# Attention: scores for the maxima six steps ahead in place of eight, and a batch's first keys rotated and split ahead of other work

## The chip, the core and the metric

The kernel runs on one core of a Trainium2 chip. Its engines each run their own instructions in order: TensorE (PE; PEld is its weight load), VectorE (DVE), ScalarE (ACT), GpSimd (POOL) and SyncE (SP), which starts transfers. They wait for one another on semaphores. The metric is the device time of one execution in microseconds (us).

## What is computed

Four blocks act on `x` (4 batches x 512 tokens x 512), each adding its result: a state-space scan, a routed ternary expert layer, cross attention, and a gated feed-forward layer with 4-bit weights. The change is in the third:

```python
q = (x @ Wq).reshape(b, n, 32, 16)          # x is the layer-normed input
k, v = jnp.split(ctx @ Wkv, 2, axis=-1)     # 512 keys a batch, 32 heads of 16
q = apply_axial_rope(q, pos_map)
k = apply_axial_rope(k, ctx_pos_map)
logits = jnp.einsum('bqhd,bkhd->bhqk', q, k) * scale
w = jax.nn.softmax(logits, axis=-1)
attn = jnp.einsum('bhqk,bkhd->bqhd', w, v)
return attn.reshape(b, n, 512) @ Wout + bout
```

## The kernel before

`stage_attention` writes one program for each engine, batch after batch; nothing is reordered later, so the order written in the code is the order in which each engine waits and works. `NT` = 4 is the number of 128-row tiles of a batch, and the 32 heads are `NG` = 8 groups of `G` = 4.

**A batch's start** (`project_next` on TensorE, `rotate_next` on VectorE, `keep_next` on ScalarE; the first batch has functions of its own). Eight projections, four of keys and four of queries, are made in the order `MIXED` and numbered `k` = 0 to 7. `project(pe, k)` (L1125 for keys, L1129 for queries) writes a bank of PSUM, `rotate(k)` (L1463 to L1467) turns it there by the positions, `high_parts(k)` (L1350) copies it as float16, `low_parts(k)` (L1471) writes what the float16 lacks, `turn_parts(k)` (L1182) transposes both, and `keep_parts(k)` (L1356) copies them to `QT` and `KT`. The queries need the rows of `x` normalised (`normalise_rows`, L1451), transposed (`turn_rows`, L1171) and copied (`keep_turned`, L1339). `project_values` (L1163) and `keep_values` (L1344) make the values.

**The steps.** A group of heads has four steps (`kt` = 0 to 3). For the softmax's maxima, `score` (L1211) multiplies queries by keys, four matmuls a step, and VectorE takes the maximum of each (L1606). When a group is complete, `keep_maxima` (L1502, L1503) writes the negated maxima in two parts, `turn_maxima` (L1217) transposes them and `send_maxima` (L1364) copies them. Then, with keys as rows, `key_scores` computes the scores again (L1234) and adds the negated maxima (L1237), two pairs a step; ScalarE takes the exponential of each pair (L1431), and `values` (L1247) multiplies by the values. After a group `keep_results` (L1372), `turn_results` (L1255) and `normalise` (L1487, L1490) finish it. The scores for the maxima run `LAG` = 2 groups, eight steps, ahead of the key scores. A batch so has eight steps with scores only, 24 with both, and eight with key scores only.

**Pieces.** The output projection of the batch before is spread over the first steps of the next: four transposes (`("turn", t)`, L1191, copied by ScalarE at L1360) and eight halves of a product (`("out", n)`, L1199, added by VectorE at L1478), twelve pieces in 16 slots of half a step each, from the first slot on. `keep_codes` (L1704) on ScalarE and `decode` (L1526 to L1528) on VectorE prepare weights of the last block.

**The ring.** Projections, scores, maxima, results and pieces share three banks of PSUM, in the order that `ring_order` lists. Before TensorE writes an item, `claim` waits until the item three places before it was consumed:

```python
of, kind, n = order[r - 3]
if kind == "proj":
    pe.wait_ge(marks[of]["lo_done"], n + 1)
elif kind == "score":
    pe.wait_ge(marks[of]["maxed"], n + 1)
elif kind == "maxima":
    pe.wait_ge(marks[of]["nmT_done"], n + 1)
elif kind == "results":
    pe.wait_ge(marks[of]["o_done"], n + 1)
```

Projection 0 of a batch is placed ahead of the last results of the batch before, so the order at a border is projection 0, results, projection 1, projection 2: projection 2 waits for `low_parts(0)`.

Of the kernel before, what the change touches and what calls it, by code (L numbers as in the profile page):

```python
# [11 lines left out]
ALU = mybir.AluOpType  # L12
ACT = mybir.ActivationFunctionType
AX = mybir.AxisListType
# [920 lines left out]
def stage_attention(nc, X, ident, ident16, gate, results, late, ins):  # L935
# [19 lines left out]
    with ExitStack() as ctx:  # L955
# [47 lines left out]
        KEYS_FIRST = tuple((s, t) for s in (KEYS, 0) for t in range(NT))  # L1003
        LAST = len(MIXED)
        FILLS = 2
        LAG = 2
        WIDE = D // 2
        PIECES = (("turn", 0), ("turn", 1), ("out", 0), ("out", 1), ("turn", 2), ("out", 2), ("out", 3), ("turn", 3),
                  ("out", 4), ("out", 5), ("out", 6), ("out", 7))
# [10 lines left out]

            return 2 * (kt // 2) + n % 2, 2 * (kt % 2) + n // 2

        def piece_at(g, kt, n, ob):

            slot = ((g + LAG) * NT + kt) * 2 + n // 2
            if ob is None or n % 2 == 0 or slot % 4 == 3 or slot // 4 * 3 + slot % 4 >= len(PIECES):
                return None
            return PIECES[slot // 4 * 3 + slot % 4]

        def ring_order(ob):  # L1030

            order = [("proj", k) for k in range(LAST)]
            for g in range(-LAG, NG + 1):
                for kt in range(NT):
                    for n in range(NT):
                        if g + LAG < NG:
                            order.append(("score", ((g + LAG) * NT + kt) * NT + n))
                        if piece_at(g, kt, n, ob):
                            order.append(piece_at(g, kt, n, ob))
                    if kt == 0 and 0 <= g + LAG - 1 < NG:  # L1040
                        order.append(("maxima", g + LAG - 1))
                    if kt == 1 and g >= 1:
                        order.append(("results", g - 1))
            return order

        order = []
# [8 lines left out]
        def batch(b, ob, run):  # L1055
# [102 lines left out]
            def on_tensor(pe):  # L1158
# [143 lines left out]
                score(0, 0, 0)  # L1302
                score(0, 0, 1)
                turn_parts(LAST - 1)
                for g in range(-LAG, NG + 1):
                    ahead, here = g + LAG < NG, 0 <= g < NG
                    for kt in range(NT):
# [3 lines left out]
                        if here:  # L1311
                            key_scores(g, kt, 0)
                        if ahead and not early:
                            score(g + LAG, kt, 1)
                        if piece_at(g, kt, 1, ob):
                            project_out(*piece_at(g, kt, 1, ob))
                        if here:
                            key_scores(g, kt, 1)
                        if ahead:
                            score(g + LAG, kt, 2)  # L1320
                        if here and kt >= 1:
                            values(g, kt - 1)
                        elif g >= 1 and kt == 0:
                            values(g - 1, NT - 1)
                        if ahead:
                            score(g + LAG, kt, 3)
                        if piece_at(g, kt, 3, ob):
                            project_out(*piece_at(g, kt, 3, ob))
                        if kt == 0 and 0 <= g + LAG - 1 < NG:
                            turn_maxima(g + LAG - 1)  # L1330
                        if kt == 1 and g == NG and b + 1 < B:
                            projects[b + 1](pe, 0)
                        if kt == 1 and g >= 1:
                            turn_results(g - 1)

            def on_scalar(act):
                def keep_turned(t):
# [62 lines left out]

                def keep_next():
                    keep_values(0)
                    keep_turned(0)
                    keep_turned(1)
                    high_parts(0)
                    keep_turned(2)
                    keep_turned(3)
                    high_parts(1)
                    for k in range(LAST):
                        keep_parts(k)  # L1410
                        if k + 2 < LAST:
# [8 lines left out]
                    keep_first()  # L1420
                else:
                    keep_next()
                for g in range(-LAG, NG + 1):
                    for kt in range(NT):
                        for pair in range(2):
                            i = (g * NT + kt) * 2 + pair
                            if 0 <= g < NG:
                                act.wait_ge(st_done, i + 1)
                                if i >= NP_:
                                    act.wait_ge(av_done, (i - NP_) // 2 + 1)  # L1430
                                nc.scalar.activation(Pr[:, i % NP_], psT[:, i % 2], ACT.Exp).then_inc(exp_done, 1)  # L1431
                            piece = piece_at(g, kt, 2 * pair + 1, ob)
                            if piece and piece[0] == "turn":
                                keep_heads(piece[1])
                        if kt == 0 and g >= 1:
                            keep_results(g - 1)
                        if kt == 0 and 0 <= g + LAG - 1 < NG:
                            send_maxima(g + LAG - 1)
                        if g == -1 and kt == 1 and b >= 1:
                            keep_codes(nc, act, late, b - 1)  # L1440
# [4 lines left out]
            def on_vector(dve, chain):  # L1445
# [58 lines left out]
                                                   op0=ALU.mult, op1=ALU.subtract).then_inc(nm_done, 1)  # L1504

                def row_stats(g):
                    if NG - LAG <= g < NG:
                        for t in range(NT + (g - NG + LAG) * 6, NT + (g - NG + LAG) * 6 + 6):
# [70 lines left out]
                    dve.wait_ge(readded, TILES)  # L1579

                def rotate_next():
                    normalise_rows(0)
                    normalise_rows(1)
                    rotate(0)
                    normalise_rows(2)
                    normalise_rows(3)
                    for k in range(LAST):
                        if k + 1 < LAST:
                            rotate(k + 1)
                        low_parts(k)  # L1590
# [4 lines left out]
                    rotate_next()  # L1595
                if b:
                    dve.wait_ge(prev["nm_done"], NG)
                for g in range(-LAG, NG + 1):
                    m = g + LAG
                    for kt in range(NT):  # L1600
                        for n in range(NT):
                            if m < NG:
                                i = (m * NT + kt) * NT + n
                                j, qt = slot_of(kt, n)
                                dve.wait_ge(scored, i + 1)
                                nc.vector.tensor_reduce(mx[:, m % 3, qt, row_order(j)], bank(("score", i)), AX.X, ALU.max).then_inc(maxed, 1)  # L1606
                            piece = piece_at(g, kt, n, ob)
                            if piece and piece[0] == "out":
                                add_projection(piece[1])
                        if kt == 1 and g >= 1:  # L1610
                            normalise(g - 1)
                        if kt == 2 and NG - LAG <= g < NG:
                            decode(g - NG + LAG)
                    if first:
                        row_stats(g)
                    if m < NG:
                        keep_maxima(m)

            def on_gpsimd(pool):
                if first:  # L1620
# [505 lines left out]
```

## Time and profile before

| what | value |
|---|---|
| median of 3 runs | 1758.98 us (1758.03 to 1761.41) |
| profiled execution | 1755.34 us, span 1753.5 us |
| TensorE, VectorE, ScalarE busy | 1487.0, 1365.2, 913.2 us |
| GpSimd busy | 690.5 us |
| maximum reductions (L1606, VectorE) | 512, 321.9 us |
| exponentials (L1431, ScalarE) | 256, 248.4 us |
| mean granted TensorE clock | 0.941 of 2.4 GHz |

Busy times are of the profiled execution. The span runs from the first to the last instruction; the profiled execution's own time is 1.8 us more. Times on a timeline are counted from the span's start. Attention's four batches have their first maximum reductions at 760.9, 917.5, 1084.6 and 1251.7 us.

### The profile page before, as it was taken

What the parts mean: (1) busy time and instruction counts of PE and PEld (TensorE: products, weight loads), DVE (VectorE), ACT (ScalarE), POOL (GpSimd) and SP (SyncE); (2) the same over time, 40 slices, a digit from 0 to 9 for tenths busy, and PEclk for the clock granted to TensorE, in tenths of its full rate; (3) what the DMA queues carried; (4) which work ended last, traced back from release to release, by engine and by line L of the source; (5) the groups of instructions that cost most, each with busy time, mean ns of one, the idle gap of its engine ahead of it and who ended that gap; (6) DMA issues with size and microseconds to landing.
All of it is one profiled execution on the core that took longest, in us unless ns stands there. A gap on an engine that the chain in (4) does not pass through costs nothing. (4 is left out here: it accounts for less than half of the span.)

```text
span 1753.5 us, 20835 instructions
## 1 busy us (share of the span) xinstructions
PE 1487.0 (85%) x6523; PEld 614.4 (35%) x6523; DVE 1365.2 (78%) x2045; ACT 913.2 (52%) x1205; POOL 690.5 (39%) x474
## 2 busy tenths in 40 slices
PE   5887997987753875689988998898899788898998
PEld 1332433432231422333344324433433333343433
DVE  6989989999988852799867966895688489665554
ACT  4766666564431100447763765476467444555464
POOL 3999999999943517200010010000000133333333
PEclk8899999998986998779999999999999899999999
DMA  7455555555658662510001000100010400000000
GB/s 245 120 151 147 136 156 151 134 145 156 160 136 219 155 123 96 198 46 1 1 1 45 1 1 1 34 1 1 1 34 1 88 12 1 24 1 24 1 24 24
DMA packets 65257, 131.51 MB, mean 75 GB/s; under 512 B 11376, under 2 KB 11376, under 8 KB 64384
## 3 DMA queue, kind: packets, MB, share of 16 engines
q1 hardware_dynamic: 53104, 104.07, 21.5%
q0 software_dynamic: 7168, 25.17, 6.3%
q10 hardware_dynamic: 4880, 0.95, 0.3%
q8 instruction: 56, 0.92, 0.2%
q14 instruction: 49, 0.40, 0.1%
HBM read 134.11 MB, written 12.85 MB: 84 GB/s over the span
## 5 line engine op out<-in xcount | busy, mean ns | idle before, releaser
L1606 DVE TENSOR_REDUCE att_mx<-att_ring 128x1 f32<-128x512 f32 x512 | 321.9, 684 | 37.7 <-PE att_ring L1211 35.4
L370 POOL TENSOR_TENSOR ssm_dBu<-ssm_du,ssm_BC 128x1024 f32<-128x1024 f32 x128 | 304.5, 2385 | 16.9 <-DVE ssm_du L406 16.9
L1431 ACT ACTIVATE att_Pr<-att_psT 128x1024 f32<-128x1024 f32 x256 | 248.4, 1023 | 105.4 <-PE att_psT L1237 104.6
L265 PE MATMUL ssm_psY<-ssm_hC,ident 128*128 128x512 f32 x512 | 254.7, 627 | 37.2 <-POOL ssm_hC L377 20.6
L334 ACT ACTIVATE ssm_dA<-ssm_delta,ssm_negA 128x512 f32<-128x512 f32 x256 | 165.4, 682 | 165.3 <-DVE ssm_hC L426 163.9
L1780 POOL TENSOR_TENSOR mlp_both<-mlp_first,mlp_third 128x512 f32<-128x512 f32 x88 | 127.8, 1453 | 225.2 <-DVE mlp_first L2014 122.9
L2014 DVE SCALAR_TENSOR_TENSOR mlp_first<-mlp_psQ,mlp_s_gu,mlp_first 128x512 f32<-128x512 f32 x176 | 131.7, 748 | 100.4 <-ACT mlp_first L1900 90.3
L471 DVE TENSOR_TENSOR_SCAN ssm_dA<-ssm_dA,ssm_dBu 128x512 f32<-128x512 f32 x148 | 178.4, 1218 | 17.8 <-ACT ssm_dA L334 13.8
L1211 PE MATMUL att_ring<-att_KT,att_QT 64*128 64x512 f16 x512 | 168.4, 393 | 17.1 <-DVE att_mx L1606 11.9
L265 PEld LDWEIGHTS ssm_psY<-ssm_hC,ident 128*128 128x128 f32 x512 | 96.0, 197 | 187.5 <-issue 94.5
L1830 PE MATMUL mlp_psD<-mlp_Wd,mlp_hT 128*128 128x512 f32 x352 | 158.3, 595 | 0.4 <-DVE mlp_Wd L1983 0.4
L1817 PE MATMUL mlp_psQ<-mlp_xh,late_Vgu 128*128 128x512 f16 x352 | 135.1, 384 | 25.5 <-DVE mlp_first L2014 19.2
L377 POOL TENSOR_TENSOR ssm_hC<-ssm_dBu,ssm_BC 128x512 f32<-128x512 f32 x108 | 142.6, 1321 | 15.3 <-DVE ssm_dBu L471 14.4
L1639 POOL TENSOR_TENSOR X<-X,late_bout 128x512 f32<-128x512 f32 x12 | 14.8, 1269 | 327.6 <-DVE att_Pr L1451 327.6
L1247 PE MATMUL att_psO<-att_Pr,att_V 128*32 128x512 f32 x1024 | 136.4, 604 | 1.4 <-ACT att_Pr L1431 1.4
L1818 PE MATMUL mlp_psQ<-mlp_xl,late_Vgu 128*128 128x512 f16 x352 | 134.7, 383 | 0.0
L1771 POOL MEMSET mlp_eps<- 128x1 f32 x1 | 0.1, 104 | 332.2 <-POOLq L65 332.2
L471 DVE TENSOR_TENSOR_SCAN ssm_dBu<-ssm_dA,ssm_dBu 128x512 f32<-128x512 f32 x108 | 129.0, 1194 | 0.0
L1234 PE MATMUL att_psT<-att_QT,att_KT 64*128 64x512 f16 x512 | 123.9, 381 | 0.3
L1237 PE MATMUL att_psT<-att_nmT,att_pick 64*128 64x512 f16 x512 | 122.7, 378 | 0.0
L897 PE MATMUL moe_psO<-moe_W,moe_XST 128*128 (+1 forms) x376 | 98.3, 388 | 24.2 <-issue 18.5
L1900 ACT ACTIVATE mlp_first<-mlp_psQ,mlp_s_gu 128x512 f32<-128x512 f32 x88 | 60.3, 685 | 101.1 <-PE mlp_psQ L1818 98.7
(272 smaller groups left out, 2314.6 us busy)
## 6 DMA issues: line engine op xcount, KB each, us to landing
ssm_BC<-bc_rows SPq DMA_DIRECT2D x128, 512.0 KB, 4.9
moe_W<-in_masksT POOLq DMA_DIRECT2D x32, 512.0 KB, 8.2
late_words<-in_gate_upT SPq DMA_DIRECT2D x32, 176.0 KB, 3.9
X<-in_x SPq DMA_DIRECT2D x4, 1024.0 KB, 10.8
rows<-moe_XP SPq DMA_DIRECT2D x4, 1024.0 KB, 14.6
out_x<-X SPq DMA_DIRECT2D x3, 1024.0 KB, 4.3
mlp_Wd<-in_downT SPq DMA_DIRECT2D x8, 352.0 KB, 9.6
ssm_ctxP<-in_ctxT SPq DMA_DIRECT2D x4, 512.0 KB, 12.3
```

The lines of the kernel that those rows point to most:

```text
L265: nc.tensor.matmul(psY[:, w, :], ident[:], hC[:, w, g % RC, :], start=False, stop=(n == DS - 1)).then_inc(summed, 1)
L334: nc.scalar.activation(dA[:, q % RA, :], delta[:, b % 2, e, :], ACT.Exp, scale=negA[:, e, n:n + 1]).then_inc(dA_done, 1)
L370: nc.gpsimd.tensor_tensor(dBu[:, g % RB], du[:, b % 2, hh * W:(hh + 1) * W, :], BC[:, g % RING, 0, :].unsqueeze(1).broadcast_to([P, W, S]) ...
L377: nc.gpsimd.tensor_tensor(hC[:, 1, g % RC, :], dBu[:, g % RB, 1, :], BC[:, g % RING, 1, :], ALU.mult).then_inc(hC_done[1], 1)
L471: nc.vector.tensor_tensor_scan(h, dA[:, q % RA, :], dBu[:, g % RB, w, :], 0.0, ALU.mult, ALU.add).then_inc(h_done, 1)
L1211: nc.tensor.matmul(out, QT[rows, pair, qt * P:(qt + 1) * P], KT[rows, pair, :], start=True, stop=True).then_inc(scored, 1)
L1247: mm = nc.tensor.matmul(psO[32 * j:32 * j + 32, :], V[:, kt, HV * (g * G + j):HV * (g * G + j) + 32], Pr[:, (i + j // 2) % NP_, j % 2, :], ...
L1431: nc.scalar.activation(Pr[:, i % NP_], psT[:, i % 2], ACT.Exp).then_inc(exp_done, 1)
L1606: nc.vector.tensor_reduce(mx[:, m % 3, qt, row_order(j)], bank(("score", i)), AX.X, ALU.max).then_inc(maxed, 1)
L1817: nc.tensor.matmul(psQ[:, g, :], Vgu[:, g, cols], xh[:, g, :], start=True, stop=False)
L1818: nc.tensor.matmul(psQ[:, g, :], Vgu[:, g, cols], xl[:, g, :], start=False, stop=True).then_inc(grp, 1)
L1830: mm = nc.tensor.matmul(psD[:, t, :], hT[:, J % HT, t * P:(t + 1) * P], Wd[:, j, :], start=(j == 0), stop=(j == JT - 1))
```

## The change

The lead of the scores for the maxima is counted in steps, no longer in groups, and is six. All engines walk the same list of steps. The maxima of a group, which were turned and sent in step 0 of a group of key scores, are turned and sent in step 2, and `keep_maxima` comes after step 1 of a group on VectorE. The pieces keep their slots counted from the first step of the batch, so the last three come in main steps 0 and 1. `keep_codes` stays three steps ahead of the first key scores, and so comes two steps earlier in the batch. At the start of batches 1 to 3 VectorE rotates projection 0 ahead of all normalisations and splits it ahead of `rotate(1)`, and ScalarE copies its high parts ahead of the turned rows.

```diff
-        LAG = 2
+        STEPS = NT * NG
+        LEAD = 6
...
+        def steps():
+            for s in range(-LEAD, STEPS + NT):
+                yield s, divmod(s, NT), divmod(s + LEAD, NT)
...
-                for g in range(-LAG, NG + 1):
-                    ahead, here = g + LAG < NG, 0 <= g < NG
-                    for kt in range(NT):
-                        early = g == -LAG and kt == 0
-                        if ahead and not early:
-                            score(g + LAG, kt, 0)
...
-                        if kt == 0 and 0 <= g + LAG - 1 < NG:
-                            turn_maxima(g + LAG - 1)
+                for s, (g, kt), (m, mk) in steps():
+                    ahead, here, early = m < NG, 0 <= g < NG, s == -LEAD
+                    if ahead and not early:
+                        score(m, mk, 0)
...
+                    if mk == 0 and 1 <= m <= NG:
+                        turn_maxima(m - 1)
...
                 def keep_next():
                     keep_values(0)
+                    high_parts(0)
                     keep_turned(0)
                     keep_turned(1)
-                    high_parts(0)
...
                 def rotate_next():
+                    rotate(0)
                     normalise_rows(0)
                     normalise_rows(1)
-                    rotate(0)
+                    low_parts(0)
+                    rotate(1)
                     normalise_rows(2)
                     normalise_rows(3)
-                    for k in range(LAST):
+                    for k in range(1, LAST):
                         if k + 1 < LAST:
                             rotate(k + 1)
                         low_parts(k)
...
+                    if mk == NT - 1 and m < NG:
+                        keep_maxima(m)
+                    if kt == 1 and g >= 1:
+                        normalise(g - 1)
```

Lines of the changed kernel are shifted by two to five in this part of the file. TensorE at the end of the steps with scores only, in batch 1, before (`late_Wout` is the output projection's half, `att_KT,att_QT` a score, `att_psT` the key scores):

```order
L1199 MATMUL att_ring<-late_Wout,late_xo 128x256 x4
L1211 MATMUL att_ring<-att_KT,att_QT 128x512 x2
L1199 MATMUL att_ring<-late_Wout,late_xo 128x256 x4
L1211 MATMUL att_ring<-att_KT,att_QT 128x512 x2
L1199 MATMUL att_ring<-late_Wout,late_xo 128x256 x4
L1211 MATMUL att_ring<-att_KT,att_QT 128x512 x3
L1234 MATMUL att_psT<-att_QT,att_KT 128x512 x2
L1237 MATMUL att_psT<-att_nmT,att_pick 128x512 x2
```

and of the change:

```order
L1216 MATMUL att_ring<-att_KT,att_QT 128x512 x3
L1239 MATMUL att_psT<-att_QT,att_KT 128x512 x2
L1242 MATMUL att_psT<-att_nmT,att_pick 128x512 x2
L1216 MATMUL att_ring<-att_KT,att_QT 128x512
L1204 MATMUL att_ring<-late_Wout,late_xo 128x256 x4
L1239 MATMUL att_psT<-att_QT,att_KT 128x512 x2
L1242 MATMUL att_psT<-att_nmT,att_pick 128x512 x2
L1216 MATMUL att_ring<-att_KT,att_QT 128x512 x2
L1204 MATMUL att_ring<-late_Wout,late_xo 128x256 x4
L1216 MATMUL att_ring<-att_KT,att_QT 128x512
L1239 MATMUL att_psT<-att_QT,att_KT 128x512 x2
L1242 MATMUL att_psT<-att_nmT,att_pick 128x512 x2
```

The halves stood between scores and now have key scores between them. VectorE in the middle of a batch, over one group, before (the maxima's two instructions, a reciprocal and the results):

```order
L1606 TENSOR_REDUCE att_mx<-att_ring 128x1 x8
L1487 RECIPROCAL att_rec<-att_ring 128x16
L1490 TENSOR_TENSOR late_heads<-att_ring,att_rec 128x4x64
L1606 TENSOR_REDUCE att_mx<-att_ring 128x1 x8
L1502 TENSOR_SCALAR att_nm<-att_mx 128x16
L1503 SCALAR_TENSOR_TENSOR att_nm<-att_mx,att_nm 128x16
```

and of the change:

```order
L1608 TENSOR_REDUCE att_mx<-att_ring 128x1 x16
L1504 TENSOR_SCALAR att_nm<-att_mx 128x16
L1505 SCALAR_TENSOR_TENSOR att_nm<-att_mx,att_nm 128x16
L1489 RECIPROCAL att_rec<-att_ring 128x16
L1492 TENSOR_TENSOR late_heads<-att_ring,att_rec 128x4x64
```

The maxima's pair moved next to the results' pair, and sixteen reductions follow in a row. VectorE at the start of batch 2, before:

```order
L1490 TENSOR_TENSOR late_heads<-att_ring,att_rec 128x4x64
L1451 TENSOR_SCALAR att_Pr<-X,att_mv,att_rstd 128x512 x2
L1463 TENSOR_TENSOR att_t_sin<-att_ring,att_table 128x512
L1464 TENSOR_TENSOR att_ring<-att_ring,att_table 128x512
L1466 TENSOR_TENSOR att_ring<-att_ring,att_t_sin 128x256
L1467 TENSOR_TENSOR att_ring<-att_t_sin,att_ring 128x256
L1451 TENSOR_SCALAR att_Pr<-X,att_mv,att_rstd 128x512 x2
L1463 TENSOR_TENSOR att_t_sin<-att_ring,att_table 128x512
L1464 TENSOR_TENSOR att_ring<-att_ring,att_table 128x512
L1466 TENSOR_TENSOR att_ring<-att_ring,att_t_sin 128x256
L1467 TENSOR_TENSOR att_ring<-att_t_sin,att_ring 128x256
L1471 TENSOR_TENSOR att_parts<-att_ring,att_parts 128x64x16
```

and of the change, from the last instruction of the first rotation on:

```order
L1469 TENSOR_TENSOR att_ring<-att_t_sin,att_ring 128x256
L1453 TENSOR_SCALAR att_Pr<-X,att_mv,att_rstd 128x512 x2
L1473 TENSOR_TENSOR att_parts<-att_ring,att_parts 128x64x16
L1465 TENSOR_TENSOR att_t_sin<-att_ring,att_table 128x512
L1466 TENSOR_TENSOR att_ring<-att_ring,att_table 128x512
L1468 TENSOR_TENSOR att_ring<-att_ring,att_t_sin 128x256
L1469 TENSOR_TENSOR att_ring<-att_t_sin,att_ring 128x256
L1453 TENSOR_SCALAR att_Pr<-X,att_mv,att_rstd 128x512 x2
```

The low parts of projection 0 (`att_parts`) stood behind two rotations and four normalisations, and stand behind one rotation and two normalisations.

## Rows read from the trace of the kernel before

**Rows 1.** Stretches of attention: length, busy us (instructions) by engine, granted clock, transfers.
```profile
775.95:781.20 5.25, 5.13 (x15) 1.52 (x16) 5.18 (x11) 0.00 (x0) 0.00 (x0) 0.50 0.00 0
781.30:787.05 5.75, 5.58 (x39) 1.91 (x37) 4.91 (x9) 4.52 (x6) 0.00 (x0) 0.74 0.01 3
...
941.60:951.00 9.40, 8.40 (x41) 5.23 (x41) 6.46 (x15) 0.65 (x2) 0.00 (x0) 1.00 0.86 211
950.40:956.25 5.85, 4.72 (x38) 1.61 (x36) 5.27 (x11) 4.47 (x5) 0.00 (x0) 1.00 0.00 0
...
974.30:986.05 11.75, 11.54 (x93) 3.90 (x88) 10.87 (x21) 8.84 (x11) 0.00 (x0) 1.00 0.01 2
1020.15:1025.00 4.85, 4.84 (x41) 1.40 (x40) 1.21 (x5) 4.75 (x6) 0.00 (x0) 1.00 0.01 3
...
1037.90:1084.60 46.70, 40.69 (x209) 20.95 (x210) 28.60 (x46) 25.41 (x31) 4.93 (x4) 0.96 0.00 1
1049.40:1054.80 5.40, 5.40 (x10) 2.33 (x11) 0.00 (x0) 0.00 (x0) 1.75 (x2) 0.68 0.00 0
```

**Rows 2.** Timeline of ScalarE, last steps: start, us, engine, line, what, count.
```profile
1022.47 0.62 ACT L1364 ACTIVATE att_nmT<-att_ring 128x512 f16<-128x512 f16 x1
1022.95 4.00 ACT L1431 ACTIVATE att_Pr<-att_psT 128x1024 f32<-128x1024 f32 x4
```

**Rows 3.** Timeline of the border between batches 1 and 2; idle time before in brackets.
```profile
1042.04 1.00 DVE L1451 TENSOR_SCALAR att_Pr<-X,att_mv,att_rstd 128x512 f32<-128x512 f32 x2
...
1042.92 0.60 PE L1171 MATMUL att_psT<-ident,att_Pr 128*128 128x128 f32 x4
...
1042.94 0.69 DVE L1463 TENSOR_TENSOR att_t_sin<-att_ring,att_table 128x512 f32<-128x512 f32 x1
...
1045.08 1.00 DVE L1451 TENSOR_SCALAR att_Pr<-X,att_mv,att_rstd 128x512 f32<-128x512 f32 x2
...
1046.21 1.02 ACT L1350 ACTIVATE att_parts<-att_ring 128x1024 f16<-128x1024 f32 x1
...
1048.12 1.22 DVE L1471 TENSOR_TENSOR att_parts<-att_ring,att_parts 128x1024 f16<-128x1024 f32 x1
...
1049.39 5.40 PE L1129 MATMUL att_ring<-att_Wq,att_xT 128*128 128x512 f32 x8 [3.71 <-DVE att_parts L1471]
...
1054.83 0.69 DVE L1463 TENSOR_TENSOR att_t_sin<-att_ring,att_table 128x512 f32<-128x512 f32 x1 [5.49 <-PE att_ring L1129]
...
1059.61 3.65 PE L1129 MATMUL att_ring<-att_Wq,att_xT 128*128 128x512 f32 x8
```

**Rows 4.** Timeline of TensorE, halves in the steps with scores only, batch 1.
```profile
944.31 1.99 PE L1199 MATMUL att_ring<-late_Wout,late_xo 128*128 128x256 f32 x8 [0.26 <-DVE X L1478]
946.23 0.39 PE L1211 MATMUL att_ring<-att_KT,att_QT 64*128 64x512 f16 x2
946.88 1.99 PE L1199 MATMUL att_ring<-late_Wout,late_xo 128*128 128x256 f32 x8 [0.26 <-DVE X L1478]
```

**Rows 5.** Timeline of VectorE in one group of batch 1.
```profile
979.20 0.25 DVE L1487 RECIPROCAL att_rec<-att_ring 128x16 f32<-128x16 f32 x1
979.48 0.42 DVE L1490 TENSOR_TENSOR late_heads<-att_ring,att_rec 128x256 f32<-128x256 f32 x1
...
985.18 0.20 DVE L1502 TENSOR_SCALAR att_nm<-att_mx 128x16 f16<-128x16 f32 x1
985.41 0.23 DVE L1503 SCALAR_TENSOR_TENSOR att_nm<-att_mx,att_nm 128x16 f16<-128x16 f32 x1
```

**Rows 6.** Instruction groups, 974.3 to 986.05: busy us, mean ns, idle before, releaser.
```profile
L1211 PE MATMUL att_ring<-att_KT,att_QT 64*128 64x512 f16 x16 | 5.3, 380 | 0.2 <-DVE att_mx L1606 0.2
```

**Rows 7.** Instruction groups, 950 to 1400, the same columns.
```profile
L1704 ACT ACTIVATE late_Vgu<-late_words 128x2816 f16<-128x2816 f16 x3 | 7.6, 2546 | 0.0
```

**Rows 8.** Timelines of VectorE and TensorE, border between batches 0 and 1.
```profile
874.04 1.00 DVE L1451 TENSOR_SCALAR att_Pr<-X,att_mv,att_rstd 128x512 f32<-128x512 f32 x2
...
881.40 6.28 PE L1129 MATMUL att_ring<-att_Wq,att_xT 128*128 128x512 f32 x8 [3.95 <-DVE att_parts L1471]
```

More of the change, by code:

```diff
@@ new lines, in on_tensor @@
+                for s, (g, kt), (m, mk) in steps():
+                    ahead, here, early = m < NG, 0 <= g < NG, s == -LEAD
+                    if ahead and not early:
+                        score(m, mk, 0)
+                    if here:
+                        key_scores(g, kt, 0)
+                    if ahead and not early:
+                        score(m, mk, 1)
+                    if piece_at(s, 1, ob):
+                        project_out(*piece_at(s, 1, ob))
+                    if here:
+                        key_scores(g, kt, 1)
+                    if ahead:
+                        score(m, mk, 2)
+                    if here and kt >= 1:
+                        values(g, kt - 1)
+                    elif g >= 1 and kt == 0:
+                        values(g - 1, NT - 1)
+                    if ahead:
+                        score(m, mk, 3)
+                    if piece_at(s, 3, ob):
+                        project_out(*piece_at(s, 3, ob))
+                    if mk == 0 and 1 <= m <= NG:
+                        turn_maxima(m - 1)
+                    if kt == 1 and g == NG and b + 1 < B:
+                        projects[b + 1](pe, 0)
+                    if kt == 1 and g >= 1:
+                        turn_results(g - 1)
@@ L1422, in on_scalar @@
                     keep_next()
[L1423 to L1440, printed above, removed]
+                for s, (g, kt), (m, mk) in steps():
+                    for pair in range(2):
+                        i = (g * NT + kt) * 2 + pair
+                        if 0 <= g < NG:
+                            act.wait_ge(st_done, i + 1)
+                            if i >= NP_:
+                                act.wait_ge(av_done, (i - NP_) // 2 + 1)
+                            nc.scalar.activation(Pr[:, i % NP_], psT[:, i % 2], ACT.Exp).then_inc(exp_done, 1)
+                        piece = piece_at(s, 2 * pair + 1, ob)
+                        if piece and piece[0] == "turn":
+                            keep_heads(piece[1])
+                    if kt == 0 and g >= 1:
+                        keep_results(g - 1)
+                    if mk == 0 and 1 <= m <= NG:
+                        send_maxima(m - 1)
+                    if g == -1 and kt == 1 and b >= 1:
+                        keep_codes(nc, act, late, b - 1)
                 if first:
@@ L1506, in row_stats @@
                 def row_stats(g):
[L1507 to L1508 removed]
+                    if NG - 2 <= g < NG:
+                        for t in range(NT + (g - NG + 2) * 6, NT + (g - NG + 2) * 6 + 6):
                             chain.mark(nc.vector.bn_stats(stats[:, t, :], X[:, t, :]))
@@ L1597, in on_vector @@
                     dve.wait_ge(prev["nm_done"], NG)
[L1598 to L1614, printed above, removed]
+                for s, (g, kt), (m, mk) in steps():
+                    for n in range(NT):
+                        if m < NG:
+                            i = (m * NT + mk) * NT + n
+                            j, qt = slot_of(mk, n)
+                            dve.wait_ge(scored, i + 1)
+                            nc.vector.tensor_reduce(mx[:, m % 3, qt, row_order(j)], bank(("score", i)), AX.X, ALU.max).then_inc(maxed, 1)
+                        piece = piece_at(s, n, ob)
+                        if piece and piece[0] == "out":
+                            add_projection(piece[1])
+                    if mk == NT - 1 and m < NG:
+                        keep_maxima(m)
+                    if kt == 1 and g >= 1:
+                        normalise(g - 1)
+                    if kt == 2 and NG - 2 <= g < NG:
+                        decode(g - NG + 2)
+                    if first and kt == NT - 1:
                         row_stats(g)
-                    if m < NG:
-                        keep_maxima(m)
             def on_gpsimd(pool):
```

44 lines of the change are left out of this document (9 added, 35 removed).

## The prediction

> **What bounds the kernel now.** The page's busy times (the table above) are averages over stages with different limits; the change touches only attention, so I read the table of stretches of attention first, then the timelines of its kinds of steps, and last the border between two batches. A step is four score matmuls with their four maximum reductions, and (in the main steps) two exponentials. A batch has three kinds of steps. In the steps ahead of the first exponential nothing but scores, maxima and the previous batch's output projection runs. Then scores and exponentials run together for 24 steps, 11.75 us for each group of four; TensorE is busy 11.54 and VectorE 10.87 of that (974.30 to 986.05) [rows 1]: both are nearly full. The last eight steps have no scores left, and ScalarE is full: four exponentials, two steps of them, start at 1022.95 and take 4.00 us [rows 2]. From 1037.9 to 1084.6 the next batch is projected, rotated and turned; TensorE is busy 40.69 of 46.7 there and VectorE 28.60 [rows 1]. The longest waits of that stretch are at its start. TensorE's third projection (L1129) waits 3.71 us for the low halves of the first keys (L1471 at 1048.12), since it writes the bank that those keys hold; VectorE's rotation of it (L1463 at 1054.83) then waits 5.49 us [rows 3]. So the batches stand in a row, and each is prologue + 24 full steps + tail + border.
>
> **The change, part A: six steps ahead.** The work of VectorE and TensorE stays the same. The last two prologue steps go, two tail steps (24 and 25) get scores, and the pieces of the output projection that stood in the last two prologue steps (three halves, `("out", 5)` to `("out", 7)`) now stand in main steps 0 and 1.
>
> Batches 1 to 3. What goes: the stretch 941.6 to 951.0, 9.4 us; main steps 0 and 1 as they were, 5.85 us (950.40 to 956.25); tail steps 24 and 25, 4.85 us (1020.15 to 1025.0) [rows 1]. Together 20.1 us. What comes:
> - Main steps 0 and 1 with three halves in them. One half occupies TensorE for 1.92 us (944.31 to the next row at 946.23), and in the prologue the next one starts 2.57 us after it (946.88 − 944.31), because its bank waits for VectorE's addition (0.26 us of it stand as a wait in the row) [rows 4]. In the main steps two key-score groups and two scores stand between halves, which cover that 0.65 us. TensorE was busy 4.72 of the 5.85 us; 4.72 + 3 × 1.92 = 10.5 us. VectorE has 5.3 + 3 × 0.34 and stays below.
> - Steps 24 and 25 at the price of a quarter group each, but they are the two heavier ones (one holds the results' transposes): I take 6.4 us against 2 × 2.94 = 5.9. The last maxima are now sent in step 26, about 0.5 us more of ScalarE there (its copy adds 0.5 us between rows 1022.47 and 1022.95) [rows 2].
> 10.5 + 6.4 + 0.5 = 17.4, so −2.7 us a batch, −8.1 for three. Bounds: if no wait between halves is covered, +3 × 0.65 a batch (−2.2 in all); if main steps take 5.5 and not 5.9 for two, −3.6 a batch (−11).
>
> Batch 0 has no halves. What goes: 5.25 (775.95 to 781.2) + 5.75 + 4.85 = 15.85 [rows 1]. What comes: two main steps in which VectorE has eight reductions and one pair of maxima, 5.3 us, + 6.9 = 12.2: −3.6 us. Against it stands the clock: from 775.95 to 781.2 TensorE was granted 0.50, which is 1.2 GHz, and over the main steps that follow (781.3 to 787.05) 0.74, so about the first 3 us of them were at the low level [rows 1]. Now they begin near 776, when the clock is still low, and TensorE, not VectorE, is the limit at that level: its 4.7 us of two such steps (4.72 in batch 1) would be up to 9.4 if the clock did not rise in them. The clock was low in the prologue and rose within 3 us of main steps. I charge 1.4 us and take −2.2 (bounds −3.6 and +0.5). The Trainium skill (TensorE: Matmul & The Clock Gate, What's actually happening) has the throttled state as the default that activity releases; by it alone the early start of the main steps brings the rise forward too. The trace agrees so far: 0.50 in the thin stretch, 0.74 in the next.
>
> The groups in between. Maxima are turned in step 2 of a group and no longer in step 0, and on VectorE the pair of maxima instructions (0.20 + 0.23 us) now stands directly ahead of the results' pair (0.25 + 0.42) [rows 5], some 1.0 us in which it frees no score bank. The ring has three banks, that is about 1.8 us of reductions; the bank of the results comes free about 0.15 us after TensorE would want it. For that the old wait after the maxima in step 0 (TensorE L1211 on L1606, 0.2 us a group) goes [rows 6], and returns in step 3. Maxima still come to TensorE one full step ahead of their use, 2.4 us or more, against two ScalarE copies. I cost it at 0, with ±0.15 us for each of some 26 groups: ±4 us.
>
> `keep_codes` on ScalarE, 2.55 us [rows 7], now stands after the third heads' copy and ahead of the fourth and of the first maxima. Those are due two prologue steps later (two such steps took 9.4 us [rows 1]), so it is hidden; if they were due at once it would cost up to 2.5 us a batch.
>
> **Part B: the first keys ahead, three borders.** Work through the border of batches 1 and 2 [rows 3]. VectorE is free at 1042.0. Rotation of the first keys takes 2.14 us (its rows 1042.94 to 1045.08) and ends at 1044.2; the two normalisations end at 1045.1. ScalarE copies the high halves from 1044.2 in 1.02 us, so the low halves run 1045.3 to 1046.6 and not from 1048.12. TensorE's first turn of rows moves from 1042.92 to about 1044.8, behind the normalisation; the second projection 1045.3 to 1047.0; the second turn to 1047.4. There the third projection starts: bank and rows are ready. It started at 1049.39: −2.0 us. Everything behind it (the normalisations of rows 2 and 3, the later rotations) has its old distance to it, since VectorE is done with them by 1050.3, ahead of the projection's end. At the first border VectorE is free at 873.9, just ahead of its normalisation at 874.04; the same distances put the third projection at 879.4 and not 881.40 [rows 8]: the same. Three borders: −6.0 us. Bounds: −1 us each (if TensorE's turns wait longer than thought) to −2.5.
>
> The clock is a second gain. The eight matmuls of that projection take 5.40 us (the stretch has a granted clock of 0.68 [rows 1]), the eight of the next query projection 3.65 (1059.61) [rows 3]; at the first border they take 6.28 [rows 8]. The fall follows TensorE's wait of 3.71 us at border two and 3.95 at border one. All of batch 1's stretches ahead of that one, with TensorE busy 8.4 of 9.4 or 4.72 of 5.85, are at 1.00 [rows 1], and 0.96 over the whole border is no more than this one fall. After the change the wait at borders two and three is some 1.7 us (1043.1 to 1044.8), at border one 2.8 (873.9 to 876.7). I count 5.40 − 3.65 = 1.75 us back at each of two borders, −3.5, and nothing at the first, where 2.6 more is to be had. The page named above says in the same section that the chip's look at activity runs free of the program, so that the same gap can fall well or badly; that is a reason not to take border one as settled, and no number here depends on it.
>
> **Sum.** −8.1 − 2.2 + 0 − 6.0 − 3.5 = −19.8 us: span 1753.5 to 1733.7. The profiled execution took 1755.3 as a whole, the median of the runs is 1759.0, 3.6 above it; from the median I come to 1739, and shade by 1 for the first border's clock: 1738. The measurement cannot tell less than about 0.2% (3.5 us) from no change.
>
> **Rivals.**
> 1. The borders gain little (10%): the row turns, now behind the rotation, hold up the third projection. TensorE's chain of turn, projection and turn from 1044.8 is in order, with no slack in it; if ScalarE's copy of rows, now behind the high halves, adds to it, the 9.5 us of part B go. Time 1748.
> 2. TensorE's halves cost their prologue price inside the main steps, or main groups lengthen by 0.15 us (12%): +4 to +6, 1743.
> 3. TensorE's busy time is modelled, and the main group is really held by the ring's turn-around, which the new spacing loosens (6%). VectorE's 10.87 is the floor, 0.88 below the group; 0.5 of that over 26 groups, −13: 1725.
> 4. Slower than before (4%): VectorE's 1.0 us between score banks stalls TensorE in every group and ScalarE's copy of the maxima then comes late for the key scores. The gain of 20 us is eaten from 0.77 us a group over 26 groups, that is if groups take over 12.5 us; at 12.7 the time is 1764. For it speaks that both engines are nearly full; against it that each has its own 0.2 to 0.9 us a group free and the bank is late by 0.15 only.
> 5. Nothing measurable (3%): the losses of 1 and 2 together with groups of 12.1.
> The forecast keeps 65%, with 1733 to 1743 as its own range. Cases 1 to 3 reach 1725 to 1748; 1730 to 1749 leaves out cases 3, 4 and 5 and little else. Faster 0.93, same 0.03, slower 0.04.
>
> **What would show it.** Part A: about 6 steps (24 reductions) ahead of a batch's first exponential, a main stretch of 26 steps of about 76 us plus the halves in batches 1 to 3, VectorE's idle time after the last reductions shorter, and first to last exponential of such a batch about 6.7 us longer than before (10.5 − 5.85 and 6.9 − 4.85). Right groups: 11.6 to 11.9 us. Wrong: TensorE's scores wait over 0.4 us a group for VectorE. Part B: TensorE's wait on the low halves of the first keys disappears, a wait of 1.7 to 2.8 us on normalised rows takes its place, VectorE's 5.49 us wait falls to about 2, and the stretch 1037.9 to 1084.6 becomes 43 long or less with granted clock 1.00 in it. What would make the forecast wrong most: groups off by more than 0.15 us.

## The result, and the profile after

The changed kernel takes 1735.51 us (median of 4 runs, 1733.61 to 1740.58), the kernel before beside it 1759.0 (1758.03 to 1761.41). The ratio is 0.987, 95% interval 0.985 to 0.989. The forecast was 1738. The profiled span went from 1753.5 to 1733.2, 20.3 us less, where the sum had 19.8.

The stretches of the kernel after that answer to [rows 1]; the columns are the same (length, then busy us of TensorE, its weight loads, VectorE, ScalarE, GpSimd, granted clock, transfers):

```profile
763.20:778.30 15.10, 14.21 (x38) 3.55 (x37) 14.86 (x27) 3.57 (x4) 0.00 (x0) 0.50 0.52 130
778.80:783.70 4.90, 4.90 (x36) 1.74 (x32) 4.32 (x8) 3.92 (x5) 0.00 (x0) 0.77 0.00 0
876.70:880.10 3.40, 3.40 (x9) 1.74 (x8) 1.91 (x4) 0.60 (x1) 0.00 (x0) 0.51 0.00 0
917.60:921.00 3.40, 3.40 (x10) 2.16 (x9) 0.70 (x3) 0.00 (x0) 0.00 (x0) 0.50 0.00 0
938.60:948.75 10.15, 10.02 (x60) 5.55 (x60) 6.29 (x12) 4.09 (x5) 0.00 (x0) 1.00 0.01 2
966.50:978.30 11.80, 11.62 (x92) 3.77 (x89) 10.96 (x21) 8.83 (x11) 0.00 (x0) 1.00 0.01 2
1013.60:1019.45 5.85, 5.85 (x47) 1.94 (x43) 5.62 (x12) 4.37 (x5) 0.00 (x0) 1.00 0.01 3
1032.50:1075.40 42.90, 38.97 (x210) 20.28 (x211) 28.79 (x47) 25.66 (x31) 4.96 (x4) 1.00 0.00 1
```

In order: batch 0's six score-only steps; its main steps 0 and 1; two stretches of low clock; batch 1's main steps 0 and 1 with the three halves (10.15 us; 10.5 were forecast); one group (11.8); steps 24 and 25 with scores (5.85; 6.4 forecast); the border of batches 1 and 2 (42.9 after 46.7, granted clock 1.00 after 0.96).

The same border in the timeline, in answer to [rows 3]:

```profile
1036.59 0.68 DVE L1465 TENSOR_TENSOR att_t_sin<-att_ring,att_table 128x512 f32<-128x512 f32 x1
...
1038.71 1.00 DVE L1453 TENSOR_SCALAR att_Pr<-X,att_mv,att_rstd 128x512 f32<-128x512 f32 x2
1039.89 1.23 DVE L1473 TENSOR_TENSOR att_parts<-att_ring,att_parts 128x1024 f16<-128x1024 f32 x1 [0.18 <-ACT att_parts L1353]
...
1045.60 0.69 DVE L1465 TENSOR_TENSOR att_t_sin<-att_ring,att_table 128x512 f32<-128x512 f32 x1 [0.74 <-PE att_ring L1134]
...
1039.31 0.66 PE L1176 MATMUL att_psT<-ident,att_Pr 128*128 128x128 f32 x4 [1.68 <-DVE att_Pr L1453]
1039.80 1.88 PE L1130 MATMUL att_ring<-att_Wkv,att_ctxT 128*128 128x512 f32 x4
...
1041.96 3.60 PE L1134 MATMUL att_ring<-att_Wq,att_xT 128*128 128x512 f32 x8
```

The low halves run at 1039.89, ahead of the third projection (L1134), which follows the second turn of rows without a wait. At this place TensorE waits once, 1.68 us for the normalised rows (1.7 were forecast), and VectorE's 5.49 us wait is 0.74 (about 2 was forecast).

The whole of attention in us, read off the two timelines: a batch is the stretch from its first maximum reduction to the end of its last exponential, a border what lies between two batches.

| | batch 0 | border | batch 1 | border | batch 2 | border | batch 3 |
|---|---|---|---|---|---|---|---|
| before | 107.8 | 48.8 | 120.4 | 46.7 | 120.4 | 46.7 | 120.4 |
| after | 104.2 | 45.6 | 119.4 | 42.9 | 117.9 | 42.9 | 117.9 |

The batches give 9.6 us, the borders 10.8. Outside this, batch 0 begins 2.3 us later and what follows attention is 2.2 shorter (370.1 to 367.9 us); no instruction there was changed, and that the two cancel is chance.

### The profile page after: what moved, and what is told of

Same layout as the page of the kernel before. It is cut to its first block and busy times, and to the rows that moved or that the text cites. A ratio compares the mean times of both kernels' runs of the same rounds, so it can differ in the third digit from the quotient of the medians.

```text
span 1733.2 us, 20835 instructions
## 1 busy us (share of the span) xinstructions
PE 1475.9 (85%) x6523; PEld 610.2 (35%) x6523; DVE 1367.6 (79%) x2045; ACT 914.4 (53%) x1205; POOL 689.2 (40%) x474
## 5 line engine op out<-in xcount | busy, mean ns | idle before, releaser
L265 PE MATMUL ssm_psY<-ssm_hC,ident 128*128 128x512 f32 x512 | 255.4, 627 | 39.5 <-DVE ssm_hC L426 19.8
L377 POOL TENSOR_TENSOR ssm_hC<-ssm_dBu,ssm_BC 128x512 f32<-128x512 f32 x108 | 142.3, 1318 | 14.7 <-DVE ssm_dBu L471 13.8
```

Of the source, the lines that this page charges most:

```text
L265: nc.tensor.matmul(psY[:, w, :], ident[:], hC[:, w, g % RC, :], start=False, stop=(n == DS - 1)).then_inc(summed, 1)
L377: nc.gpsimd.tensor_tensor(hC[:, 1, g % RC, :], dBu[:, g % RB, 1, :], BC[:, g % RING, 1, :], ALU.mult).then_inc(hC_done[1], 1)
```

## Experiments

In the table, border one is that between batches 0 and 1, border and batch are batch 2 and the border ahead of it, and group is a middle group of batch 1; these four columns are of the one profiled execution of each run. Each median was taken with the kernel before on the same chip, where that had 1757.0 to 1757.8 us (1759.0 beside the changed kernel), and the ratio is to it. Medians of different rows can come from different chips, so gains are compared below as each kernel's distance from the kernel before beside it: 23.5 us for the changed kernel.

One part of the spread is not of attention. Its first maximum reduction comes between 760.6 and 767.2 us in the 13 profiled executions, though nothing ahead of it was edited. The three latest (766.4 in the border alone, 767.0 in the wait filled with seven, 767.2 in the results first) had TensorE at 1.2 GHz for 173.6 us before that point, the other ten (760.6 to 763.7) for 143.4 to 163.8 us.

| run | median us | ratio (95%) | border one | border | batch | group |
|---|---|---|---|---|---|---|
| before | 1757 to 1759 | | 48.8 | 46.7 | 120.4 | 11.76 |
| changed | 1735.5 | 0.987 (0.985 to 0.989) | 45.6 | 42.9 | 117.9 | 11.81 |
| lead alone | 1744.0 | 0.993 (0.992 to 0.995) | 49.0 | 46.7 | 117.8 | 11.81 |
| border alone | 1746.8 | 0.994 (0.992 to 0.996) | 45.6 | 42.9 | 120.4 | 11.76 |
| lead of 7 | 1733.7 | 0.987 (0.985 to 0.989) | 43.9 | 42.9 | 118.0 | 11.62 |
| lead of 5 | 1743.2 | 0.993 (0.991 to 0.995) | 44.2 | 42.9 | 120.6 | 12.03 |
| pieces ahead | 1732.9 | 0.987 (0.985 to 0.989) | 45.6 | 42.9 | 117.1 | 11.81 |
| results first | 1726.4 | 0.983 (0.981 to 0.985) | 43.9 | 42.9 | 117.6 | 11.52 |
| VectorE's order alone | 1746.9 | 0.995 (0.993 to 0.996) | 50.2 | 47.8 | 117.9 | 11.81 |
| wait filled, 7 | 1757.2 | 1.000 (0.999 to 1.001) | 48.0 | 47.1 | 120.4 | 11.76 |
| wait filled, 4 | 1754.5 | 0.998 (0.998 to 0.999) | 46.2 | 45.0 | 122.0 | 11.76 |
| both | 1726.8 | 0.982 (0.981 to 0.984) | 43.9 | 42.9 | 116.9 | 11.52 |
| both, lead of 7 | 1733.0 | 0.987 (0.986 to 0.989) | 43.9 | 42.9 | 117.7 | 11.62 |

**The parts apart.** The lead alone undoes the order at the border:

```diff
@@ the changed kernel, rotate_next
-                    rotate(0)
                     normalise_rows(0)
                     normalise_rows(1)
-                    low_parts(0)
-                    rotate(1)
+                    rotate(0)
...
-                    for k in range(1, LAST):
+                    for k in range(LAST):
```

with `keep_next` as before; the border alone has `LEAD = 8`.

> Part A alone: six steps of lead, the border between batches as in the kernel before. If the two parts add up, the batches keep their measured gain (3.5 us in batch 0, about 2.4 in each of the others, 10.7 in all) and the borders take 46.8 us from the last exponential to the next batch's first maximum reduction: a median of about 1748. The rival, that the border's gain hangs on the shorter lead (TensorE and VectorE reach the border in another state), would show borders other than 46.8 and 48.9 us.

> Part B alone: lead of eight steps, the first keys rotated and split ahead. If the parts add up, the borders take 42.9 us at borders two and three and about 45.6 at the first (11.1 us gained in all), the batches 120.3 us from first reduction to last exponential as before: a median of about 1748. If the first border's smaller gain belongs to the first batch's end (VectorE's row statistics come out later with the short lead), this run shows a larger gain there.

Both came out: the lead alone has the changed kernel's batches (104.2, 117.8) and the old borders, the border alone the reverse. They gave 13.8 and 11.0 us, 24.8 together, and the change 23.5 on its own chip. In the first run the median moved more than the batches' 11.2 us; its four runs spread from 1741.5 to 1747.7.

**How far the lead can go** (`LEAD = 7`, `LEAD = 5`).

> Changed kernel with a lead of seven steps. If the gain of part A is overlap of score-only steps with tail steps, it is about half of it: 5 us above the changed kernel, about 1741, with 7 steps ahead of the first exponential. If the gain came from where in a group the maxima are turned (step 2 in place of step 0), then step 1, together with the results on TensorE and ScalarE, is a place of its own and groups would move by tenths of a us from 11.8.

> Changed kernel with a lead of five steps: the maxima are turned at the end of the step right ahead of their use. Theory: ScalarE then has the step's two exponentials and the copy of the maxima to do before TensorE's key scores can start, and TensorE waits some 1 us in each of 32 groups; groups of 12.8 us, a median near 1763, slower than the changed kernel. This is the mechanism of the prediction's slower rival. The rival here: there is still room, groups stay at 11.8, and one more step saves 1 to 2 us a batch: about 1731.

Neither time was right. One group with seven steps, then one with five:

```profile
965.75:977.37 11.62, 11.41 (x90) 3.78 (x88) 10.91 (x21) 8.85 (x11) 0.00 (x0) 1.00 0.01 2
```

```profile
964.26:976.30 12.04, 11.72 (x90) 3.75 (x88) 10.97 (x20) 8.81 (x11) 0.00 (x0) 1.00 0.01 2
```

Seven steps are as fast as six. Batch 0 takes 105.0 us, 0.8 more than with six, but a group takes 11.62 us in place of 11.81, and only one half of the output projection stands in a main step. So the place of the maxima in a group is worth 0.19 us a group, as the second theory had it, and the gain of the lead does not grow evenly. Five steps cost 0.22 us a group and not 1: TensorE's key scores wait for ScalarE's copy of the maxima, by this row of its waits from 960 to 1010 (what, total us, times, longest),

```profile
PEld att_psT L1239 <- ACT att_nmT L1367: 1.6, 4, 0.4
```

0.4 us of wait once a group, with a group 0.22 us longer. The slower rival's mechanism exists, and begins between six and five steps; with five the kernel is still 0.7% faster than before.

**What holds a group at 11.81 us.** The timeline of the changed kernel in answer to [rows 5], and TensorE's wait from 960 to 1010:

```profile
1007.25 0.20 DVE L1504 TENSOR_SCALAR att_nm<-att_mx 128x16 f16<-128x16 f32 x1
1007.49 0.23 DVE L1505 SCALAR_TENSOR_TENSOR att_nm<-att_mx,att_nm 128x16 f16<-128x16 f32 x1
1007.60 0.25 DVE L1489 RECIPROCAL att_rec<-att_ring 128x16 f32<-128x16 f32 x1
1007.88 0.42 DVE L1492 TENSOR_TENSOR late_heads<-att_ring,att_rec 128x256 f32<-128x256 f32 x1
```

```profile
PE att_ring L1216 <- DVE late_heads L1492: 0.9, 5, 0.2
```

A score waits some 0.2 us in each group for the bank of the results, which the maxima's pair delays. The run swaps the two:

```diff
+                    if kt == 1 and g >= 1:
+                        normalise(g - 1)
                     if mk == NT - 1 and m < NG:
                         keep_maxima(m)
-                    if kt == 1 and g >= 1:
-                        normalise(g - 1)
```

> Changed kernel, but VectorE finishes a group's results ahead of writing the maxima's two parts. If the bank of the results, held while VectorE writes the maxima, is what makes a group 11.81 us with six steps of lead and not 11.62 as with seven, groups fall by 0.1 to 0.2 us and the median by 3 to 5: about 1731. If TensorE's own work and the order of its waits for the values bind, the groups stay at 11.81 and the time within 1 us. A loss is possible too: VectorE may then wait for the results with the maxima's parts behind them.

The group falls to 11.52 us, under that of the kernel before:

```profile
965.40:976.90 11.50, 11.50 (x90) 3.80 (x88) 10.77 (x21) 8.83 (x11) 0.00 (x0) 1.00 0.01 2
```

TensorE is busy all of it, and the wait is gone from the list. The cause was as expected and its size was not: 0.29 us a group where 0.1 to 0.2 were expected. The wait accounts for 0.2 of that; the rest stays open. The median is 30.5 us under the kernel before beside it, 7.0 more than the changed kernel's 23.5. The batches explain 6 of these (1.5 us each, first to last exponential), a first border without a low-clock stretch could be another 1.7 (45.6 to 43.9 us). The profiled execution itself was slower than the other three of this kernel (1733.8 us against 1726.3 to 1726.5): its first projection comes 4.7 us later than the changed kernel's, and batches 2 and 3 each have a low-clock stretch of their own at 1.2 us (117.6 us, where batch 1 takes 116.4). The ratios' intervals just meet here, and stand apart in the run of both finds below. This is the largest gain that the experiments added to the change: two adjacent blocks of VectorE work, 1.1 us in all, in the other order.

**The halves in the main steps.** All pieces in the first twelve half-step slots:

```diff
-            if ob is None or n % 2 == 0 or slot % 4 == 3 or slot // 4 * 3 + slot % 4 >= len(PIECES):
+            if ob is None or n % 2 == 0 or slot >= len(PIECES):
                 return None
-            return PIECES[slot // 4 * 3 + slot % 4]
+            return PIECES[slot]
```

> Changed kernel, but the twelve pieces of the output projection take twelve consecutive half-step slots, so all of them stand in the six score-only steps and none in main steps 0 and 1. Theory: a half costs TensorE 1.7 to 1.9 us in the full main steps and about as much more (2.57 us from one to the next) where two follow each other in the score-only steps; main steps 0 and 1 fall from 10.15 to about 4.9 us, the six steps ahead grow from 24 to about 29: the same within 1 us a batch, a median of 1732 to 1738. The rival, that pieces are nearly free in the score-only steps (9 of them added 9.0 us to 6 steps), gives 27 us for the six steps and 2 us less a batch: 1729.

The six steps and the two after them:

```profile
1071.90:1100.60 28.70, 24.95 (x131) 15.94 (x129) 18.80 (x35) 7.44 (x10) 0.00 (x0) 1.00 0.22 51
1100.60:1105.20 4.60, 4.38 (x35) 1.29 (x32) 4.37 (x8) 3.86 (x5) 0.00 (x0) 1.00 0.00 0
```

28.7 + 4.6 us in place of 24.0 + 10.15: three halves cost 1.85 us each in the main steps, close to TensorE's full price (1.92 in the forecast), and 1.57 in the steps ahead. That is 0.8 us a batch and 2.4 in all in the trace, inside what the theory allowed. The medians do not show it: the distance from the kernel before is 24.0 us here and 23.5 for the changed kernel, the same ratio.

**The order on one engine only.** The changed kernel with ScalarE's `high_parts(0)` behind `keep_turned(1)`.

> Changed kernel, but ScalarE copies the first keys' high halves behind the first two turned rows, as before. The two halves of part B hang together: VectorE's low halves stand ahead of its second rotation and wait for ScalarE, which now waits for TensorE's second turn of rows. Theory: TensorE's third projection starts some 3 us later, the borders take about 46 us and the median is near 1744, that is most of part B gone. The rival, that the order on VectorE alone carries the gain, keeps 42.9 us.

```profile
1041.34 0.65 PE L1176 MATMUL att_psT<-ident,att_Pr 128*128 128x128 f32 x4 [1.68 <-DVE att_Pr L1453]
...
1047.01 5.40 PE L1134 MATMUL att_ring<-att_Wq,att_xT 128*128 128x512 f32 x8 [2.86 <-DVE att_parts L1473]
```

The third projection starts 5.67 us after the first turn of rows and not 2.65, and is slow again (5.40 us): the clock falls in or behind a wait of 2.86 us here, at all three borders. The border is 47.8 us, 1.1 worse than before, and more than the 46 expected. VectorE's half of part B alone is a loss. ScalarE's half alone was not run.

**Is it the clock?** In the kernel before, extra matmuls fill the wait:

```diff
                     turn_rows(1)
+                    for _ in range(7):
+                        nc.tensor.matmul(psT[:, 1, 1, :], ident[:], Wkv[:, 0, 0:D], start=True, stop=True)
                     project(pe, 2)
```

> Kernel before with seven extra matmuls (identity by a slice of a weight, into a bank that is rewritten later, their result unused) at the place where TensorE waits 3.7 us for the first keys' low halves, at each of three borders. They take 3.0 us and fit into the wait. If the fall of the clock in that wait is what makes the third projection take 5.40 us, it now takes 3.65 at granted clock 1.00: borders two and three fall by 1.75 us, the first by up to 2.6, and the median by 5 to 6 us to about 1752. If the matmuls were slow for another reason (the operands, the bank), nothing changes.

> As the run with seven extra matmuls, with four. Seven took 6.17 us (each of them is two passes of 0.43 us, and I had counted one), so they outlasted the wait by 2.5 us; four take 3.4 us and fit into 3.7. If the wait's fall of the clock is the cause of the 5.40 us, the third projection of keys and queries (eight matmuls) starts where it did before and takes 3.6: borders two and three 45.0 us in place of 46.7, the first some 46, a median about 5 us under the kernel before: 1752. If not, 1757.

Seven were too many: they took 6.17 us, and the projection behind them started 2.5 us late. It still took 3.60 us. Four fit (timeline, then stretches, of that run):

```profile
1045.69 3.60 PE L1287 MATMUL att_psT<-att_Wkv,ident 128*128 128x512 f32 x8
1049.57 3.70 PE L1129 MATMUL att_ring<-att_Wq,att_xT 128*128 128x512 f32 x8 [0.27 <-DVE att_parts L1473]
```

```profile
1049.57:1053.10 3.53, 3.53 (x8) 1.57 (x9) 0.00 (x0) 0.00 (x0) 1.78 (x2) 1.00 0.00 0
1087.40:1090.80 3.40, 3.40 (x8) 2.50 (x8) 0.96 (x2) 0.00 (x0) 0.00 (x0) 0.50 0.00 0
```

The projection takes 3.70 us at granted clock 1.00, and the borders 45.0 and 46.2, as the clock theory has it: 1.7 and 2.6 us. The operands and the bank of the projection are as they were, so its slowness was the clock's. But the median fell by 2.8 us (interval 1.2 to 4.4) and not 5. In the profiled execution batches 2 and 3 each have 3.4 us at 1.2 GHz in their second score-only step (the second row), which makes them 122.0 us and takes 3.3 of the borders' 6.0 us back. That fits the median, but it is one execution; and since such stretches come in runs without any filling too (below), it is not shown that the filling brought them.

**The two finds together** (results first, pieces ahead), with six and with seven steps.

> Changed kernel with the results finished ahead of the maxima's parts, and all twelve pieces in the score-only steps. The two gains should add: groups 11.52 us (1.4 us a batch less), the batches 1 to 3 from first reduction to last exponential about 115.7 us and batch 0 102.7: 8 us less than the changed kernel in all, a median of 1727 or a little less. If the pieces' gain only stood against the held bank of the results, it would be near 1730.

> The same with seven steps of lead. There the maxima's parts and the results are in different steps of a group, the group took 11.62 us, and a step more stands ahead alone. If overlap decides, it is about 1 us a batch slower than with six: batches of 116.5 to 117, a median of 1729 to 1731. If the score-only steps have room that a seventh gives to the pieces (14 slots for 12), it is equal.

Both gains are in the batches: 102.6 us and, in batches 1 and 3, 115.6, as expected (116.9 in batch 2, with 3.4 us of low clock). The median, 1726.8, is 30.5 us under the kernel before (ratio 0.982), 7.0 more than the changed kernel's distance, but that is also the distance of the results first alone; whether the pieces' 2.4 us are in it can't be told from these runs. With seven steps the pieces ahead gain 0.3 us a batch, and the group stays at 11.62.

## Why the prediction was right

The time, its direction and the mechanism of both parts were right. That the sum came within a microsecond (20.3 of span for 19.8) is partly luck: batches 1 to 3 gave 2.1 us less than forecast, batch 0 1.4 more and the borders 1.3 more, and these cancel. By the terms of the sum:

- **Batches 1 to 3, −8.1 forecast.** Measured −2.5 in batches 2 and 3, −1.0 in batch 1, where 3.4 us at 1.2 GHz in the second score-only step (the row 917.60:921.00) cost 1.5. Its parts: the halves in main steps 0 and 1, 10.15 for 10.5; steps 24 and 25, 5.85 for 6.4, so my surcharge for the heavier steps was wrong; but main steps 2 and 3 now take 5.9 and not 5.1 us (step 2 holds the turning and sending of maxima that stood in step 0), which I had not counted, and the first exponential comes 8.9 us earlier in a batch and not 9.4. The 0.5 us charged for step 26 came as 0.1.
- **Batch 0, −2.2.** Measured −3.6, the value without my charge for the low clock. Main steps 0 and 1 ran at granted clock 0.77, no lower than the 0.74 they had before [rows 1], and took 4.90 us. The stretch at 1.2 GHz ends at 781.1 us after 784.2, 3.1 us earlier, and the first exponential comes 2.5 us earlier, so my charge of 1.4 us was wrong. The section of the Trainium skill that the prediction cited (TensorE: Matmul & The Clock Gate, What's actually happening) states activity as what releases the clock, and the trace agrees with it here: the rise moved with the main steps.
- **Groups, 0.** 11.81 after 11.76. I had the wait for the results' bank at 0.15 us and it was 0.2, and named it; that swapping two blocks takes it away I did not see.
- **Borders, −6.0 and −3.5 of clock,** which is −3.75 at each of borders two and three and −2.0 at the first. Measured −3.8 and −3.8, and −3.2 at the first. The replay by rows was right to 0.1 us (TensorE's wait of 1.68 us, the third projection 2.65 us after the first turn of rows). At the first border the forecast left out the clock, and the profiled execution has a low-clock stretch there, shorter than before:

```profile
875.26 0.66 PE L1176 MATMUL att_psT<-ident,att_Pr 128*128 128x128 f32 x4 [2.65 <-DVE att_Pr L1453]
875.75 2.73 PE L1130 MATMUL att_ring<-att_Wkv,att_ctxT 128*128 128x512 f32 x4
```

  The wait is 2.65 us (2.8 forecast) and the projection behind it slow (2.73 for 1.88). The same border took 43.9 us without a low-clock stretch in four of the eight profiled executions with this order, 44.2, also without one, in the run with five steps, and 45.6 with one in three. Nothing in the edits tells the two kinds apart, and the 1 us that the forecast took off for it was a guess.

Of the rivals, the first (ScalarE's copies of rows hold up the border) did not come: the third projection follows the second turn of rows without a wait. The run with ScalarE's old order is not this rival but its reverse, the high halves held up by the copies. The second (halves at their score-only price) did not either: 1.85 us, not 2.57. The third was right in part: the ring did hold the group, by 0.2 to 0.3 us and not 0.5, but the new spacing tightened it, and only the swap loosened it. The fourth, slower, needs the copy of the maxima to be late, which is so with five steps, at 0.22 us a group and not 0.77.

## What to carry to other kernels

Where the stages of a loop are bound by different engines, moving whole steps from the thin ends into the middle pays only for what the full engine has left. Each moved instruction is costed at that engine's full price, which held here to 0.1 us for each half. Where a shared ring of banks is released by an in-order engine, put the work that frees a bank ahead of the work that nobody waits for yet. A reordering across engines is made on every engine of the chain: with VectorE's half alone the borders were worse than with none.

## What the runs showed of the hardware

At borders two and three a wait of TensorE of 2.86 or 3.7 us was followed by 3.4 us at 1.2 GHz each time (six borders in three profiled executions; 5.40 us for eight matmuls that take 3.60). Where the longest wait of the border was 1.68 us it was followed by none (16 borders in eight executions). At the first border one of 2.65 us was followed by it in the changed kernel and three more executions, and not in four others; and one of 2.94 us, with five steps, was not:

```profile
875.86 0.66 PE L1176 MATMUL att_psT<-ident,att_Pr 128*128 128x128 f32 x4 [2.94 <-DVE att_Pr L1453]
```

So the length of the one wait does not settle it. Filling the wait with matmuls kept 2.4 GHz at all six borders of the two runs.

Not expected was a second place: 4.3 to 5.1 us behind a batch's first maximum reduction, in the second score-only step, 3.4 us at 1.2 GHz come in 8 of the 39 batches behind a border: batch 1 of the changed kernel, batch 3 of the border alone, batches 2 and 3 of the results first, batch 2 of both finds, batch 1 of the wait filled with seven, and batches 2 and 3 of that filled with four, of which the first is this. They cost 1.2 to 1.7 us each:

```profile
1086.06 0.66 PE L1191 MATMUL att_ring<-ident,late_heads 128*128 128x128 f32 x4 [1.16 <-ACT late_xo L1362]
...
1087.40 3.65 PE L1199 MATMUL att_ring<-late_Wout,late_xo 128*128 128x256 f32 x8 [0.36 <-ACT late_xo L1362]
```

The half (L1199) takes 3.65 us where [rows 4] has 1.99. TensorE had waited 1.16 us for ScalarE's copy of the heads just before, as it also does in batch 1 of the kernel before, where no low clock follows:

```profile
920.48 0.66 PE L1191 MATMUL att_ring<-ident,late_heads 128*128 128x128 f32 x4 [1.16 <-ACT late_xo L1360]
...
921.82 1.99 PE L1199 MATMUL att_ring<-late_Wout,late_xo 128*128 128x256 f32 x8 [0.36 <-ACT late_xo L1360]
```

The same code is hit or missed. The Trainium skill (TensorE: Matmul & The Clock Gate, What's actually happening) says that the look at activity runs free of the program, which fits both places; no run here moved it on purpose, so that part is argued and not shown. If it is so, a gain from the clock at one place, such as the border's, can be partly given back at another by chance, and single executions and small sets of runs can't separate that from an edit.
